# Two attentions reordered: first attention in steps of two tiles with full-row maxima, second attention's transposes one tile later

## The chip, the cores and the metric

The kernel runs on one core of a Trainium2 chip. The metric is the device time of one execution in microseconds (us). Three runs of the kernel before took 2622.91 to 2623.58 us, median 2623.57 us. Engines: TensorE (PE, its weight loads PEld), VectorE (DVE), ScalarE (ACT), GpSimd (POOL) and SyncE (SP), which here issues the DMAs.

## The reference

Two layers, each a cross attention and a feed-forward block, are added to x (16 batches of 56 queries, 256 wide), with a context of 1500 rows of 128 per batch. The two attentions are what the change touches:

```python
    # layer 0: 16 heads of 16; the last 16 context rows go to a second small attention
    q = _ln((x @ Wq + bq).reshape(b, s1, H, HD), qn_w, qn_b)
    k, v = _ln(kv[..., :HD], kn_w, kn_b), kv[..., HD:]
    s = jnp.einsum('bhqd,bhkd->bhqk', q, k) * SCALE
    ctx = jnp.einsum('bhqk,bhkd->bhqd', jax.nn.softmax(s, axis=-1), v)
    # layer 1: 16 heads of 128, rmsnorm on q and k
    scores = jnp.einsum('bqhd,bkhd->bhqk', rmsnorm(q, gq), rmsnorm(k, gk)) * scale
    out = jnp.einsum('bhqk,bhkd->bhqd', jax.nn.softmax(scores, axis=-1), v)
x = x + xattn0(layernorm(x), ctx); x = x + moe(layernorm(x))
x = x + xattn1(layernorm(x), ctx); x = x + bitlinear_ffn(layernorm(x))
```

## The kernel before

The kernel is one program of phases: keys and values of the first attention (and key norms of the second), queries, the first attention (`phase_attention0`), a mixture of experts, the second attention (`phase_attention1`), and a quantised feed-forward block. Each engine has its own instruction stream, written out by hand; semaphores order them. An engine takes its instructions strictly in the written order, so the order of the Python code is the order on the engine. In both attentions one batch is one step; a step has 12 tiles of 128 context rows (`NK`, the last tile is shorter), and 896 columns are the 16 heads times 56 queries, in two halves of 448. fp32 operands are split into a rounded high part and a low rest, so one product of scores is three matmuls per half.

**First attention.** For tile s of batch p, TensorE does six score matmuls into two PSUM banks `sc` (`scores`, lines 1338 to 1340, each half waits until the exp of the tile before has left its bank), ScalarE takes the exp into one of three buffers `pr` (line 1398), and TensorE multiplies the tile two back with the values (`products`, line 1350, 16 heads, 17 columns of weights each). The softmax needs each query's maximum before its scores are made, so while batch p is worked on TensorE computes for batch p+1 a first, coarse product of the rounded queries and keys (`maxima`, line 1312), which VectorE reduces (line 1453). Its 24 matmuls come in 12 groups of two, and the table `PRE` says after which tile's scores which groups stand. Head pairs lie in four sets of 32 rows; each maxima matmul contracts only its own 32 rows, since the queries `QH` are zero in the others. At tile 9 VectorE makes a diagonal of the maxima, TensorE spreads it (`max_rows`, line 1320), and VectorE adds it to the queries (line 1486). ScalarE also rounds batch p+1's keys in three chunks, behind the exps of tiles 0, 1 and 2 (line 1388). The steps run from p = -2 to 16; p = 1 to 12 are a hardware loop over pairs (`Fori`) on every engine, the others are written out (`run`, line 1264).

**Second attention.** For batch b and tile j TensorE makes the scores into a ring of four PSUM banks (`ring`, line 982), VectorE scales them by the key norms into `S` (line 1106) and keeps a running maximum `mx` (lines 1127 and 1130). When tile 11 is done, TensorE transposes `mx` in two parts of 4 and 3 blocks (`maxima`, line 1009), VectorE reduces them (line 1114) and splits them, TensorE spreads them over all rows into two ring banks (`spread`, line 1024), ScalarE copies them to `mb` (line 1173), and GpSimd subtracts them from the 12 tiles (line 1150), ScalarE takes the exps (line 1179), and TensorE multiplies with the context (`output`, line 994). All of this for batch b runs during step b+1, its last six tiles' outputs even in step b+2: at tile j of step b stand, in this order, the scores of b, the first part of the transposes of b-1 (j = 0), an output of b-2 (j < 5), the second part (j = 0), the spreading (j = 1), and an output of b-1 (j > 5). Steps 2 to 13 are a loop over pairs.

The lines that place the maxima of both attentions:

```python
    PRE = {1: (0,), 2: (1, 2), 3: (3,), 4: (4, 5), 5: (6,), 6: (7, 8), 7: (9,), 8: (10, 11)}
    ...
                    if back and j == 0:
                        maxima(0)
                    ...
                    if back and j == 0:
                        maxima(1)
                    if back and j == 1:
                        spread()
```

Of the kernel before, what the change touches and what calls it, by code (L numbers as in the profile page):

```python
# [27 lines left out]
P = 128  # L28
# [5 lines left out]
NK = 12  # L34
# [843 lines left out]
def phase_attention1(nc, g):  # L878
# [15 lines left out]
    with ExitStack() as ctx:  # L894
# [5 lines left out]
        mx, mb = sb("mx", [P, HQ]), sb("mb", [P, HQ])  # L900
# [58 lines left out]
        def _(pe):  # L959
            def step(b, pair, i, front, nxt, back, end):  # L960
                def scores(j):
# [4 lines left out]
                    for half in range(2):  # L966

                        use = 2 * j + half + (2 if j >= 2 else 0)
                        r = (USES * i + use) % RING

                        if use < 4:
                            if from_(b, 1):
                                pe.wait_ge(s_scaled, SC * b - 3 + use)
                        elif use in (8, 9):
                            if from_(b, 1):
                                pe.wait_ge(mb_ready, 2 * (b - 1) + use - 7)
                        else:
                            pe.wait_ge(s_scaled, SC * b + (use - 4 if use < 8 else use - 6) + 1)
# [21 lines left out]
                def maxima(k):  # L1000
# [7 lines left out]
                    for q in range(lo, hi):  # L1008
                        mm = pe.transpose(tb[:, (q - lo) * P:(q - lo + 1) * P], mx[:, q * P:(q + 1) * P], g.ident[:, :])
                    mm.then_inc(mT_ready, 1)  # L1010

                def spread():
# [3 lines left out]
                    for half in range(2):  # L1016
                        if front:
                            pe.wait_ge(s_scaled, SC * b + half + 1)
                        r = (USES * i + 4 + half) % RING
# [51 lines left out]
        def _(dve):  # L1071
# [8 lines left out]

            def step(b, pair, i, front, nxt, back, end):
                for j in range(NK):
# [16 lines left out]
                    if front:  # L1099
                        if from_(b, 2):  # L1100
                            dve.wait_ge(p_used, NK * (b - 2) + j + 1)
                        for half in range(2):
                            r = (USES * i + 2 * j + half + (2 if j >= 2 else 0)) % RING
# [6 lines left out]
                    if back and j == 0:  # L1110

                        for k, (lo, hi) in enumerate(TI):
                            dve.wait_ge(mT_ready, 2 * (b - 1) + k + 1)
                            dve.tensor_reduce(mcol[:, lo:hi],
                                              tb[:, 0:(hi - lo) * P].rearrange("p (a n) -> p a n", n=P),
                                              X, ALU.max).then_inc(mT_taken, 1)
# [6 lines left out]
                    if front:  # L1123

                        dve.wait_ge(s_scaled, SC * b + 2 * j + 2)
                        if j == 0:
                            dve.tensor_copy(mx[:, :], S[i][:, 0, :]).then_inc(mx_ready, 1)
                        else:
                            dve.wait_ge(mx_ready, NK * b + j)
# [1257 lines left out]
```

## Time and profile before

| | |
|---|---|
| median of 3 runs | 2623.57 us |
| profiled execution | 2625.33 us, span 2623.6 us |
| granted TensorE clock, mean | 0.903 of full speed |
| TensorE busy | 2223.8 us (85%) |
| VectorE busy | 1781.6 us (68%) |
| GpSimd busy | 1236.7 us (47%) |
| ScalarE busy | 1187.0 us (45%) |
| first attention, first to last score matmul | about 913 to 1391 us |
| second attention | about 1724 to 2455 us |

The table sums the whole program; its stages have different limits, so each attention is read by itself. Busy time of TensorE is the time in which a matmul is in flight, and matmuls overlap: the distance of two starts is what one costs. A granted clock of 1.00 is 2.4 GHz, 0.50 is 1.2 GHz.

### The profile page before, as it was taken

Reading aid. Unit: us, or ns where it says so; the run is one execution under the profiler, and the core shown is the slowest. Engines: PE = TensorE matmul, PEld = TensorE weight load, DVE = VectorE, ACT = ScalarE, POOL = GpSimd, SP = SyncE. Lnnn points to the kernel's source line nnn. Section 1 sums busy time; section 2 is a strip of 40 time slices with the busy share of each in tenths; the row PEclk is TensorE's granted clock in tenths of the full one; section 3 lists DMA queues with packets and bytes.
Section 4 is the critical chain, followed back from the end, with each engine's and each line's share of the span. In section 5 each row is a group of like instructions: output and inputs, shape, how many; then the busy total and the mean of one; then the engine's idle time right before and its main releaser. Section 6 shows DMA issues by size and latency. Waiting matters only on the chain. (4 is left out here: it accounts for less than half of the span.)

```text
span 2623.6 us, 47067 instructions
## 1 busy us (share of the span) xinstructions
PE 2223.8 (85%) x16760; PEld 1749.7 (67%) x16760; DVE 1781.6 (68%) x2275; ACT 1187.0 (45%) x2007; POOL 1236.7 (47%) x988
## 2 busy tenths in 40 slices
PE   6999999999954599999996776958898989898675
PEld 4887888787832476666674343448888888888543
DVE  5878888888855465555552336968888888887057
ACT  5888888888820154445451123513232323233202
POOL 5666666666510243333330211318686868687300
PEclk9999999999976599999998687979898989899887
DMA  3232323232213133222220622241121212120500
GB/s 99 111 143 109 142 109 142 109 139 113 120 54 86 69 117 113 103 105 103 103 77 31 205 80 75 86 121 50 50 98 49 98 49 98 49 99 20 208 5 14
DMA packets 93876, 246.16 MB, mean 94 GB/s; under 512 B 19409, under 2 KB 65394, under 8 KB 84450
## 3 DMA queue, kind: packets, MB, share of 16 engines
q1 hardware_dynamic: 87602, 231.17, 24.6%
q10 hardware_dynamic: 4608, 9.44, 0.9%
q0 software_dynamic: 1536, 3.67, 0.5%
q8 instruction: 99, 1.62, 0.2%
q14 instruction: 31, 0.25, 0.0%
HBM read 144.25 MB, written 100.01 MB: 93 GB/s over the span
## 5 line engine op out<-in xcount | busy, mean ns | idle before, releaser
L1150 POOL TENSOR_TENSOR a_S<-a_S,a_mb 128x896 f32<-128x896 f32 x192 | 523.2, 2762 | 218.3 <-ACT a_mb L1173 218.3
L317 DVE TENSOR_REDUCE rk<-n_sq 128x1024 f32 (+2 forms) x384 | 465.6, 1213 | 129.3 <-ACT n_sq L255 126.9
L255 ACT ACTIVATE n_sq<-n_slot 128x1024 f32<-128x1024 f32 (+1 forms) x384 | 394.3, 1027 | 140.3 <-PE n_slot L211 131.8
L994 PEld LDWEIGHTS a_ob<-a_y,a_S 128*128 128x128 f32 (+1 forms) x2688 | 346.8, 203 | 6.9 <-issue 1.9
L994 PE MATMUL a_ob<-a_y,a_S 128*128 128x129 f32 (+1 forms) x2688 | 349.8, 286 | 1.7 <-issue 1.7
L209 PE MATMUL n_slot<-n_wh,n_yh 128*128 128x512 f32 (+1 forms) x768 | 318.3, 414 | 25.1 <-POOL n_yl L153 25.1
L1453 DVE TENSOR_REDUCE a_mpart<-a_pre 112x2 f32<-112x1024 f32 (+1 forms) x192 | 219.1, 1178 | 176.1 <-PE a_pre L1312 176.0
L1398 ACT ACTIVATE a_pr<-a_sc 128x448 f32<-128x448 f32 (+1 forms) x384 | 208.3, 544 | 249.7 <-PE a_sc L1340 238.8
L1179 ACT ACTIVATE a_S<-a_S 128x896 f32<-128x896 f32 x192 | 181.1, 950 | 271.1 <-POOL a_S L1150 270.7
L211 PE MATMUL n_slot<-n_wh,n_yl 128*128 128x512 f32 (+1 forms) x768 | 303.7, 395 | 0.0
L210 PE MATMUL n_slot<-n_wl,n_yh 128*128 128x512 f32 (+1 forms) x768 | 302.0, 393 | 0.0
L1130 DVE TENSOR_TENSOR a_mx<-a_mx,a_S 128x896 f32<-128x896 f32 (+1 forms) x176 | 286.8, 1630 | 18.0
L1106 DVE TENSOR_TENSOR a_S<-a_ring,rk 128x448 f32<-128x448 f32 (+1 forms) x384 | 221.6, 612 | 28.8 <-PE a_ring L984 28.8
L183 POOL TENSOR_TENSOR n_khat<-n_kb,n_rs 128x240 f32<-128x240 f32 x192 | 114.3, 595 | 234.5 <-DVE n_rs L332 234.4
L1408 POOL TENSOR_TENSOR a_kl<-a_kT,a_kh 128x1024 fp32r<-128x1024 f32 (+1 forms) x48 | 109.9, 2313 | 213.8 <-ACT a_kh L1388 213.8
L982 PE MATMUL a_ring<-a_Qh,a_yh 128*128 128x448 f32 (+1 forms) x384 | 160.8, 419 | 39.5 <-DVE a_S L1106 24.9
L1338 PE MATMUL a_sc<-a_QM,a_kh 128*128 128x448 f32 (+1 forms) x384 | 164.5, 428 | 19.0 <-issue 18.1
L209 PEld LDWEIGHTS n_slot<-n_wh,n_yh 128*128 128x128 f32 (+1 forms) x768 | 143.1, 186 | 51.3 <-issue 25.0
L211 PEld LDWEIGHTS n_slot<-n_wh,n_yl 128*128 128x128 f32 (+1 forms) x768 | 142.8, 186 | 35.0
L210 PEld LDWEIGHTS n_slot<-n_wl,n_yh 128*128 128x128 f32 (+1 forms) x768 | 143.8, 187 | 26.5
L170 POOL TENSOR_TENSOR n_kb<-n_kb,n_kbias 128x256 f32<-128x256 f32 x192 | 141.6, 737 | 9.7 <-ACT n_kb L269 9.7
L1339 PE MATMUL a_sc<-a_QL,a_kh 128*128 128x448 f32 (+1 forms) x384 | 143.7, 374 | 0.0
(336 smaller groups left out, 4043.6 us busy)
## 6 DMA issues: line engine op xcount, KB each, us to landing
vdram<-n_v SPq DMA_DIRECT2D x16, 1632.0 KB, 5.3
a_v<-vdram SPq DMA_DIRECT2D x16, 1632.0 KB, 6.9
kTdram<-n_kT SPq DMA_DIRECT2D x16, 1484.0 KB, 5.0
a_kT<-kTdram SPq DMA_DIRECT2D x16, 1484.0 KB, 6.5
n_yT<-in_ctxT SPq DMA_DIRECT2D x16, 750.0 KB, 8.9
yhdram<-n_yh SPq DMA_DIRECT2D x16, 750.0 KB, 6.4
yldram<-n_yl SPq DMA_DIRECT2D x16, 750.0 KB, 8.5
a_yh<-yhdram SPq DMA_DIRECT2D x16, 750.0 KB, 6.6
```

The source lines that it names most:

```text
L209: pe.matmul(dst, high, wh[:, cols], start=True, stop=False)
L210: pe.matmul(dst, high, wl[:, cols], start=False, stop=False)
L211: mm = pe.matmul(dst, low, wh[:, cols], start=False, stop=True)
L255: act.activation(sq[0:n, w, :], slot[w][0:n, :], ACT.Square).then_inc(slot_free, 1)
L317: dve.tensor_reduce(g.rk[0:n, b, j, 8 * s:8 * s + 8], sq[0:n, (2 * j + s) % 3, :].rearrange("p (h d) -> p h d", h=8), X, ALU.add)\
L994: mm = pe.matmul(ob[k][:, (q - lo) * (C + 1):(q - lo + 1) * (C + 1)], S[k_][0:n, j, q * P:(q + 1) * P], y1[k_][0:n, j, :], start=(j == 0 a ...
L1106: dve.tensor_tensor(S[i][0:n, j, half * HALF:(half + 1) * HALF].rearrange("p (h q) -> p h q", h=8), ring[r][0:n, 0:HALF].rearrange("p (h q ...
L1130: dve.tensor_tensor(mx[0:n, :], mx[0:n, :], S[i][0:n, j, :], ALU.max).then_inc(mx_ready, 1)
L1150: pool.tensor_tensor(S[1 - i][0:n, j, :], S[1 - i][0:n, j, :], mb[0:n, :], ALU.subtract)\
L1179: act.activation(S[1 - i][0:n, j, :], S[1 - i][0:n, j, :], ACT.Exp).then_inc(p_ready, 1)
L1398: act.activation(pr[0:n, s % 3, unit, :], sc[unit][0:n, 0:HALF], ACT.Exp).then_inc(p_ready, 1)
L1453: dve.tensor_reduce(mpart[:, chunk, k:k + 2], pre[group % 2][0:QP, :, 0:hi - lo], X, ALU.max).then_inc(pre_max, 1)
```

## The change

In the second attention the two parts of the transposes stand one tile later on TensorE, behind the scores of tile 1 (the first ahead of the output, the second behind it), and the spreading stands at tile 2. VectorE reduces them at tile 1. `mx` has two buffers; the copy of tile 0 into it is gone, and the first maximum is taken over tiles 0 and 1 at once, between the two reductions. The ring banks that the spreading takes move two uses on.

In the first attention TensorE's step goes over the tiles in pairs: both tiles' scores, the groups of maxima, then the products of the two tiles before. Three tables (`BETWEEN` the scores, `BEHIND` them, `LAST` behind the products) place the 12 groups. Each maxima matmul contracts all 128 rows. `pr` has four buffers. TensorE's steps are all written out in Python instead of a loop over pairs; the other engines keep theirs. The wait for the shifted queries is made for each half.

```diff
-        mx, mb = sb("mx", [P, HQ]), sb("mb", [P, HQ])
+        mx, mb = two("mx", [P, HQ]), sb("mb", [P, HQ])
...
-                    if back and j == 0:
+                    if back and j == 1:
                         maxima(0)
                     if end and j < LAG:
...
-                    if back and j == 0:
+                    if back and j == 1:
                         maxima(1)
-                    if back and j == 1:
+                    if back and j == 2:
                         spread()
...
+                    if back and j == 1:
+                        reduced(b, 0)
+                    if front and j == 1:
+                        dve.wait_ge(s_scaled, SC * b + 4)
+                        dve.tensor_tensor(mx[i][:, :], S[i][:, 0, :], S[i][:, 1, :], ALU.max).then_inc(mx_ready, 2)
+                    if back and j == 1:
+                        reduced(b, 1)
...
-                        if j == 0:
-                            dve.tensor_copy(mx[:, :], S[i][:, 0, :]).then_inc(mx_ready, 1)
...
-    PRE = {1: (0,), 2: (1, 2), 3: (3,), 4: (4, 5), 5: (6,), 6: (7, 8), 7: (9,), 8: (10, 11)}
+    BETWEEN = {6: (6, 7)}
+    BEHIND = {0: (0, 1), 2: (2, 3), 4: (4, 5), 8: (10, 11)}
+    LAST = {6: (8, 9)}
...
-        pr = sb("pr", [P, 3, 2, HALF])
+        pr = sb("pr", [P, 4, 2, HALF])
...
-                    mm = pe.matmul(pre[group % 2][0:QP, n, 0:hi - lo], QH[i][32 * r:32 * r + 32, half, r * QP:(r + 1) * QP],
-                                   kh[i][32 * r:32 * r + 32, half, lo:hi], start=True, stop=True)
+                    mm = pe.matmul(pre[group % 2][0:QP, n, 0:hi - lo], QH[i][:, half, r * QP:(r + 1) * QP],
+                                   kh[i][:, half, lo:hi], start=True, stop=True)
...
+                for s in range(0, NK, 2):
                     if held(p):
                         scores(p, i, s)
+                    groups(p, i, BETWEEN.get(s, ()))
+                    if held(p):
+                        scores(p, i, s + 1)
...
+                    groups(p, i, BEHIND.get(s, ()))
+                    for j in (s - PV, s - PV + 1):
+                        if s >= PV and held(p):
+                            products(p, i, pair, j)
...
+                    groups(p, i, LAST.get(s, ()))
...
-            run(pe, step)
+
+            for p in range(-2, B + 1):
+                step(p, p % 2, p // 2)
...
-                            if unit == 0 and later(t - 2):
-                                act.wait_ge(p_used, t - 2)
+                            if unit == 0 and later(t - 3):
+                                act.wait_ge(p_used, t - 3)
```

On VectorE in the second attention, at the start of a step, before: `a_S<-a_ring` is the scaling of two halves, `a_mx` the running maximum, `a_mcol<-a_tb` the reduction of a transposed part, `a_mh` and `a_ml` its split.

```order
L1130 TENSOR_TENSOR a_mx<-a_mx,a_S 92x896
L1106 TENSOR_TENSOR a_S<-a_ring,rk 128x448 x2
L1114 TENSOR_REDUCE a_mcol<-a_tb 128x4
L1114 TENSOR_REDUCE a_mcol<-a_tb 128x3
L1120 CAST a_mh<-a_mcol 128x7
L1122 TENSOR_TENSOR a_ml<-a_mcol,a_mh 128x7
L1127 COPY a_mx<-a_S 128x896
L1106 TENSOR_TENSOR a_S<-a_ring,rk 128x448 x2
L1130 TENSOR_TENSOR a_mx<-a_mx,a_S 128x896
```

The same place after the change:

```order
L1132 TENSOR_TENSOR a_mx<-a_mx,a_S 92x896
L1112 TENSOR_TENSOR a_S<-a_ring,rk 128x448 x4
L1084 TENSOR_REDUCE a_mcol<-a_tb 128x4
L1120 TENSOR_TENSOR a_mx<-a_S 128x896
L1084 TENSOR_REDUCE a_mcol<-a_tb 128x3
L1126 CAST a_mh<-a_mcol 128x7
L1128 TENSOR_TENSOR a_ml<-a_mcol,a_mh 128x7
```

The scaling of tile 1 moved ahead of the reductions, the copy is gone, and a maximum stands between the two reductions.

On TensorE in the second attention, a step's start before: `a_ring` are score matmuls (the last half of tile 0), `a_tb` the transposes, `a_ob` an output.

```order
L982 MATMUL a_ring<-a_Qh,a_yh 128x448
L983 MATMUL a_ring<-a_Ql,a_yh 128x448
L984 MATMUL a_ring<-a_Qh,a_yl 128x448
L1004 REGISTER_ALU
L1006 REGISTER_ALU
L1009 MATMUL a_tb<-ident,a_mx 128x128 x4
L990 ISA
L994 MATMUL a_ob<-a_y,a_S 128x129 x7
L1002 ISA
L1009 MATMUL a_tb<-ident,a_mx 128x128 x3
L973 REGISTER_ALU
L982 MATMUL a_ring<-a_Qh,a_yh 128x448
```

After, from the same half of tile 0 on:

```order
L984 MATMUL a_ring<-a_Qh,a_yl 128x448
L990 ISA
L994 MATMUL a_ob<-a_y,a_S 128x129 x7
L973 REGISTER_ALU
L982 MATMUL a_ring<-a_Qh,a_yh 128x448
L983 MATMUL a_ring<-a_Ql,a_yh 128x448
L984 MATMUL a_ring<-a_Qh,a_yl 128x448
L982 MATMUL a_ring<-a_Qh,a_yh 128x448
L983 MATMUL a_ring<-a_Ql,a_yh 128x448
L984 MATMUL a_ring<-a_Qh,a_yl 128x448
L1004 REGISTER_ALU
L1006 REGISTER_ALU
```

An output and the scores of tile 1 now stand between tile 0's scores and the wait for the last maximum; the transposes follow.

On TensorE in the first attention, one tile before: `a_sc` scores, `a_pre` a group of maxima, `a_ob` products, the last row the denominators.

```order
L1338 MATMUL a_sc<-a_QM,a_kh 128x448
L1339 MATMUL a_sc<-a_QL,a_kh 128x448
L1340 MATMUL a_sc<-a_QM,a_kl 128x448
L1338 MATMUL a_sc<-a_QM,a_kh 128x448
L1339 MATMUL a_sc<-a_QL,a_kh 128x448
L1340 MATMUL a_sc<-a_QM,a_kl 128x448
L1307 REGISTER_ALU
L1312 MATMUL a_pre<-a_kh,a_QH 112x512 x2
L1343 REGISTER_ALU
L1350 MATMUL a_ob<-a_pr,a_v 17x56 x16
L1357 MATMUL a_ob<-a_osum,a_den 128x224
```

After, the second tile of a pair up to the denominators:

```order
L1343 MATMUL a_sc<-a_QM,a_kh 128x448
L1344 MATMUL a_sc<-a_QL,a_kh 128x448
L1345 MATMUL a_sc<-a_QM,a_kl 128x448
L1343 MATMUL a_sc<-a_QM,a_kh 128x448
L1344 MATMUL a_sc<-a_QL,a_kh 128x448
L1345 MATMUL a_sc<-a_QM,a_kl 128x448
L1316 MATMUL a_pre<-a_kh,a_QH 112x512 x4
L1355 MATMUL a_ob<-a_pr,a_v 17x56 x32
L1362 MATMUL a_ob<-a_osum,a_den 128x224
```

Two groups of maxima stand in one run, and two tiles' products behind them; the register instructions of the loop are gone.

## Rows read from the trace of the kernel before

**Rows 1.** Stretches: us, then busy us (instructions) of each engine, granted clock, DMA share, GB/s.
```profile
1790.00:2379.00 589.00, 520.63 (x3541) 496.95 (x3542) 498.77 (x623) 187.86 (x224) 438.15 (x159) 0.92 0.20 71
1884.00:1890.00 6.00, 4.36 (x21) 4.37 (x22) 3.27 (x4) 0.95 (x1) 0.56 (x1) 0.50 0.00 0
1032.60:1061.20 28.60, 28.24 (x510) 20.43 (x498) 17.74 (x18) 15.77 (x28) 11.10 (x8) 1.00 0.33 118
```

**Rows 2.** SP's issues in order: start us, us, engine, line, operation, tiles.
```profile
974.72 0.33 SPq L1217 DMA_DIRECT2D a_v<-vdram  x1
...
1286.98 0.33 SPq L1217 DMA_DIRECT2D a_v<-vdram  x1
...
1315.60 0.33 SPq L1217 DMA_DIRECT2D a_v<-vdram  x1
```

**Rows 3.** Waits, first attention: who waited for whom: total us, times, longest.
```profile
PEld a_sc L1338 <- issue: 18.9, 5, 4.1
```

**Rows 4.** TensorE in order, first attention; brackets: idle time before, and its releaser.
```profile
1037.05 0.47 PE L1338 MATMUL a_sc<-a_QM,a_kh 128*128 128x448 f32 x1
1037.36 0.37 PE L1339 MATMUL a_sc<-a_QL,a_kh 128*128 128x448 f32 x1
...
1038.18 0.36 PE L1340 MATMUL a_sc<-a_QM,a_kl 128*128 128x448 f32 x1
1038.47 0.49 PE L1312 MATMUL a_pre<-a_kh,a_QH 32*112 32x512 f32 x4
1038.89 0.59 PE L1350 MATMUL a_ob<-a_pr,a_v 128*17 128x56 f32 x32
1039.41 0.47 PE L1338 MATMUL a_sc<-a_QM,a_kh 128*128 128x448 f32 x1
...
1040.82 0.48 PE L1312 MATMUL a_pre<-a_kh,a_QH 32*112 32x512 f32 x2
...
1057.93 1.06 PE L1320 MATMUL a_pre<-a_dm,a_sel 112*128 112x112 f32 x8
...
1064.88 0.74 PE L1338 MATMUL a_sc<-a_QM,a_kh 128*128 128x448 f32 x1 [3.49 <-issue]
```

**Rows 5.** ScalarE in order, first attention.
```profile
1037.97 1.15 ACT L1398 ACTIVATE a_pr<-a_sc 128x448 f32<-128x448 f32 x2 [0.26 <-PE a_sc L1340]
```

**Rows 6.** TensorE in order, second attention, around a step's start.
```profile
1885.64 1.11 PE L1009 MATMUL a_tb<-ident,a_mx 128*128 128x128 f32 x4 [3.84 <-DVE a_mx L1130]
1886.54 3.22 PE L994 MATMUL a_ob<-a_y,a_S 128*128 128x129 f32 x14
1889.55 0.85 PE L1009 MATMUL a_tb<-ident,a_mx 128*128 128x128 f32 x3
...
1891.56 1.72 PE L994 MATMUL a_ob<-a_y,a_S 128*128 128x129 f32 x14
1893.03 0.31 PE L1024 MATMUL a_ring<-a_identr,a_mh 128*128 128x128 f32 x1
```

**Rows 7.** VectorE in order, second attention, same stretch.
```profile
1883.82 1.69 DVE L1130 TENSOR_TENSOR a_mx<-a_mx,a_S 92x896 f32<-92x896 f32 x1
...
1886.79 0.69 DVE L1114 TENSOR_REDUCE a_mcol<-a_tb 128x4 f32<-128x512 f32 x1 [0.21 <-PE a_tb L1009]
1890.44 0.56 DVE L1114 TENSOR_REDUCE a_mcol<-a_tb 128x3 f32<-128x384 f32 x1 [2.96 <-PE a_tb L1009]
...
1891.32 0.62 DVE L1127 COPY a_mx<-a_S 128x896 f32<-128x896 f32 x1
...
1893.14 1.09 DVE L1130 TENSOR_TENSOR a_mx<-a_mx,a_S 128x896 f32<-128x896 f32 x1
1895.82 1.23 DVE L1106 TENSOR_TENSOR a_S<-a_ring,rk 128x448 f32<-128x448 f32 x2 [1.58 <-PE a_ring L984]
```

**Rows 8.** GpSimd in order, second attention, one batch.
```profile
1851.30 33.26 POOL L1150 TENSOR_TENSOR a_S<-a_S,a_mb 128x896 f32<-128x896 f32 x12 [11.05 <-ACT a_mb L1173]
```

**Rows 9.** Waits, second attention.
```profile
POOL a_S L1150 <- ACT a_mb L1173: 133.3, 12, 11.2
```

More of the change, by code:

```diff
@@ L966, in scores @@
                     for half in range(2):
-                        use = 2 * j + half + (2 if j >= 2 else 0)
+                        use = 2 * j + half + (2 if j >= 3 else 0)
                         r = (USES * i + use) % RING
@@ L1017, in spread @@
                         if front:
-                            pe.wait_ge(s_scaled, SC * b + half + 1)
-                        r = (USES * i + 4 + half) % RING
+                            pe.wait_ge(s_scaled, SC * b + half + 3)
+                        r = (USES * i + 6 + half) % RING
                         for q in range(3 * half, 4 + 3 * half):
@@ L1170, in step @@
                     for half in range(2):
-                        r = (USES * i + 4 + half) % RING
+                        r = (USES * i + 6 + half) % RING
                         act.wait_ge(mb_psum, 2 * (b - 1) + half + 1)
@@ L1324, in prob @@
             def prob(h, j):
-                return pr[:, j % 3, h // 8, (h % 8) * NQ:(h % 8 + 1) * NQ]
+                return pr[:, j % 4, h // 8, (h % 8) * NQ:(h % 8 + 1) * NQ]
             def scores(b, i, j):
@@ L1329, in scores @@
                 if j == 0:
-                    pe.wait_ge(qm_ready, 2 * b + 2)
                     pe.wait_ge(ql_built, 2 * b + 2)
@@ L1334, in scores @@
                 for half in range(2):
+                    if j == 0:
+                        pe.wait_ge(qm_ready, 2 * b + half + 1)
                     if later(2 * t + half - 1):
@@ L1362, in _, with groups @@
             pe.wait_ge(ob_zero, 2)
+            def groups(p, i, which):
+                if held(p + 1):
+                    for group in which:
+                        maxima(p + 1, 1 - i, group)
             def step(p, i, pair):
-                for s in range(NK):
+                for s in range(0, NK, 2):
                     if held(p):
                         scores(p, i, s)
+                    groups(p, i, BETWEEN.get(s, ()))
+                    if held(p):
+                        scores(p, i, s + 1)
                     if s == NK - 2 and held(p + 1):
                         max_rows(p + 1)
-                    if held(p + 1):
-                        for group in PRE.get(s, ()):
-                            maxima(p + 1, 1 - i, group)
-                    if s >= PV and held(p):
-                        products(p, i, pair, s - PV)
-                    if s < PV and held(p - 1):
-                        products(p - 1, 1 - i, pair - 1 + i, s - PV + NK)
-                    if s == PV + 1 and held(p - 1):
+                    groups(p, i, BEHIND.get(s, ()))
+                    for j in (s - PV, s - PV + 1):
+                        if s >= PV and held(p):
+                            products(p, i, pair, j)
+                        if s < PV and held(p - 1):
+                            products(p - 1, 1 - i, pair - 1 + i, j + NK)
+                    groups(p, i, LAST.get(s, ()))
+                    if s == PV and held(p - 1):
                         denominators(p - 1, 1 - i)
-            run(pe, step)
+            for p in range(-2, B + 1):
+                step(p, p % 2, p // 2)
         @block.scalar
@@ L1455, in step @@
             def step(p, i, pair):
-                for s in range(NK):
-                    if held(p + 1):
-                        for group in PRE.get(s, ()):
-                            maximum(p + 1, group)
+                for s in range(0, NK, 2):
                     if s == PV and held(p - 1):
@@ L1467, in step @@
                         dve.reciprocal(rec[:, :], ob[1 - i][:, 4 * NQ:8 * NQ]).then_inc(rec_ready, 1)
-                    if s == NK - 3 and held(p + 1):
+                    if held(p + 1):
+                        for group in BETWEEN.get(s, ()) + BEHIND.get(s, ()) + LAST.get(s, ()):
+                            maximum(p + 1, group)
+                    if s == NK - 2 and held(p + 1):
                         b = p + 1
```

30 lines of the change are left out of this document (14 added, 16 removed).

## The prediction

> **What bounds the kernel now.** I read the table by stretches first, then the chain of waits of the two attentions, then the instructions in order of time. In the second attention no engine is full: TensorE is busy 521 of 589 us and VectorE 499 [rows 1]. POOL's twelve subtractions take 33.26 us behind 11.05 us of idle time, so one batch takes 44.3 us [rows 8]. What closes that cycle is seen around the step's start. VectorE ends the last running maximum of a batch at 1885.51 (1883.82 + 1.69) [rows 7]; TensorE has idled 3.84 us for it [rows 6], then transposes it, runs 14 product matmuls and transposes the rest; VectorE idles 2.96 us for these and 1.58 us for the scores behind them [rows 7]. The reader is to see that VectorE's idle time, not its work, is what is paid, and that TensorE's idle time brings a second price: at 1884 to 1890 the granted clock is 0.50 (1.2 GHz) [rows 1], and 14 product matmuls last 3.22 us there against 1.72 us a few us later [rows 6].
>
> In the first attention TensorE is busy 28.24 of 28.60 us at a granted clock of 1.00 [rows 1]: it is the bound, and each instruction taken from it or added to it counts. A batch takes 28.60 us in the steps written out at the end (1286.98 to 1315.60), but the ten batches from 974.72 to 1286.98 take 312.26 us [rows 2], which is 26 us more than ten times 28.6. The waits say why: five times TensorE waits for nothing that the profile shows, 18.9 us in all [rows 3], and the matmul behind such a wait lasts 0.74 us against 0.47 us elsewhere [rows 3, 4], the lower clock. All five are at the return of TensorE's loop over pairs of batches.
>
> **First attention, loop.** The changed kernel writes TensorE's 19 steps out. The five returns go: -26 us. Code written out as such cost nothing in the last steps (28.60 us), so I charge nothing for it. What is late next is ScalarE's, VectorE's and GpSimd's own loop return, which lay inside TensorE's gap and shows no price there. Ends: 26 us gained, or nothing if another engine's return takes the same time; I take 26, since in the second attention all engines return through loops too, and GpSimd's idle time before a batch is 133.3 us over twelve, 11.2 us the longest [rows 9]: none is longer for a return.
>
> **First attention, order and maxima.** I build a step from the intervals of [rows 4] (start to start):
> - Scores: 0.205 us per matmul ((1038.18 - 1037.36) / 4), 72 of them, 14.8 us, before and after. Coming from products costs 0.10 more (0.31 against 0.205), leaving for another tile shape 0.08 more (0.29 against 0.205). Before, each is paid 12 times, 2.2 us; after, the entry 7 times (the two groups placed behind the products at step 6 pay one) and the exit 6 times, 1.2 us.
> - Products: 0.52 us for a tile's block (1038.89 to 1039.41). Before 12 blocks, 6.2 us. After, two tiles in one run; the second adds 0.52 less a change of shape, about 0.40: 5.5 us.
> - Maxima: before, 32-row matmuls lie beside each other: four last 0.49 us, two 0.48, and the next block starts 0.42 us after them. Eight such blocks cost 3.3 us, and VectorE's reductions hold one up by 0.4 us. After, 24 matmuls of all 128 rows follow each other. No row has this one. The lower end is a quarter of a block of four, 0.10 us; the upper is the 112-column matmul of line 1320, 1.06 us for 8, stretched to 512 columns, 0.61 us. I take the scores' 0.205 us for 448 columns, the same rows and type: 0.23 us at 512, 0.21 us at 460, in all 5.4 us.
> - Maxima rows and denominators: 1.0 and 0.3 us, unchanged.
> - New wait: the second tile's scores stand right behind the first's and use the same two PSUM banks, so they wait for its exp. That starts 0.92 us after the scores and takes 0.55 us [rows 4, 5], so ends at 1.47 us; the second tile would start at 1.34 us. With the load exposed again (0.10 us) that is 0.3 us (ends 0 and 0.4) for five of six pairs (maxima stand between at step 6): 1.4 us. Everything on TensorE is queued behind it, products and maxima too. In the first pair the maxima want the first rounded keys, which ScalarE makes between two exps: 0.3 us.
> Sum before: 14.8 + 2.2 + 6.2 + 3.3 + 0.4 + 1.3 = 28.2 us (28.60 in the trace). Sum after: 14.8 + 1.2 + 5.5 + 5.4 + 1.3 + 1.7 = 29.9 us. A step is 1.4 us longer after keeping part of the 0.4 us that my sum misses; 15 steps carry maxima: +21 us. VectorE's 12 reductions and SP's loads have slack there (VectorE 17.74 of 28.60 us busy [rows 1]), so their later places cost nothing; the fourth probability buffer lets ScalarE run one tile further and is needed for the pairs.
>
> What row tiling is worth bears on this sum. Two 32-row matmuls last as long as four (0.48 and 0.49 us), so half of the blocks used half of it. The Trainium skill (TensorEngine Tiling, Theoretical Speedup) gives up to fourfold for a contraction of 32 or less. By that rule the old maxima would be worth a quarter of 5.4 us, and the edit would cost 4.1 us a step instead of 1.7 us net of the stall; by the rows old blocks cost 3.7 us. The trace does not agree with the full factor, so the sum keeps the rows.
>
> **Second attention.** Times count from the end of the last maximum (1885.51), with the rows of before as durations.
> - Before, VectorE does until tile 2's scaling (1895.82, 10.3 us): scaling of tiles 0 and 1, 1.2 each (1891.94, the copy's end, to 1893.14), reductions 0.69 and 0.56, rounding 0.3 (1891.00 to 1891.32), copy 0.62, maximum 1.09, and idle 0.21 + 2.96 + 1.58; together 10.4 [rows 7].
> - After, TensorE has products and tile 1's scores in the time in which it idled (they need 1.5 us, from 1891.56 to 1893.03, and 6 x 0.205 = 1.2 us, of 3.84), and transposes at once at full clock. VectorE has two scalings (2.4), reduction 0.69, maximum over tiles 0 and 1 (1.09, on the other buffer, so it may stand between the reductions), reduction 0.56, rounding 0.3: 5.0 us without a wait. The copy, 0.62 us, is gone.
> - What is late next: TensorE waits about 1 us for the first reduction before transposing the rest (VectorE is through with it at 3.1 us), then tile 2's scores to 4.9, products 1.5, spreading the maxima (16 small matmuls between 1893.03 and tile 2's scores, which VectorE has at 1895.82, so 1.9 us with 0.9 us for the half tile and its way; it now stands behind tile 2's scores), then tile 3's scores, whose first half is ready at 9.2 us. VectorE would be ready at 7.3 us (5.0 + 1.2 + 1.09) and idles 2 us. Before, tile 3 was scaled at 10.3 + 1.2 + 1.5 = 13.0 us, the 1.5 between the maximum's 1.09 and 1.69, since GpSimd starts in it. A step gains 3.8 us.
> - GpSimd starts at about 9 us instead of 10.1 (1851.30 and one batch of 44.3) and needs 33.3 us of a 40.5 us batch. TensorE is busy 39 of 44.3 us now (521 of 589) and gets back the 3 us or so of its slow stretch (its 14 products alone 1.5 us): some 37 us. Neither is the bound.
> 15 batches (all that have a tile 1 of their own beside maxima of the one before) gain 3.8 us, 57 us. TensorE's gap of 3.84 us becomes two of about 1 us; I take it that the clock stays up, and A is the case in which it doesn't.
>
> **Sum.** -26 + 21 - 57 = -62 us. The profiled execution took 2625.33 us with a span of 2623.6; 2563 us for it. It lies 1.8 us above the runs' median, 2623.57, so about 2561 us.
>
> **Rivals.**
> A, the second attention keeps its slow stretch or its contention. For it: VectorE's maximum is 1.69 us while GpSimd works and 1.09 us while it doesn't [rows 7], and GpSimd starts earlier in the step. If the clock still falls, TensorE's products and spreading take 1.5 to 2 us longer and tile 3 comes as much later; a step gains 1.9 us: 15 x 1.9 less, 2590 us. Against: TensorE's longest gap shrinks to about 1 us. That two-input VectorE work contends with GpSimd is also in the Trainium skill (GPSIMD Engine Reference, Specifications); by that rule, the trace agrees.
> B, the pairs cost nothing: the exp is not late, and a first-attention step comes to 28.4 us. -26 - 3 - 57: 2538 us. Against: 1.47 is over 1.34.
> C, the five returns stay in another form, because ScalarE or VectorE is then late at its own return: 2587 us. For it: before, they return in the shade of TensorE. Against: the second attention, as above.
> D, slower: the 128-row maxima run near the rate of line 1320. Place: the maxima matmuls of the first attention; price 24 of them a step. A step changes by 24 g - 3.9 us for g us each, the saved 83 us are 5.5 us over 15 steps, so from g = 0.39 us on the kernel is slower; at 0.61 us it is 15 x 10.7 - 83 = +78: 2701 us. For it only row 1320; against, the scores at 0.205 us.
> E, no change to be measured: the gain of the second attention needs TensorE's work to move before the wait; if tile 1's scores still ended behind it, only copy and loop would go, -9 - 26 + 21: 2609 us, still faster. Only a mix with D gives no change.
>
> **How the numbers follow.** Forecast 50%, A 18%, B 15%, C 9%, D 3%, E and mixtures 5%. The forecast's own range is 2548 to 2576 (exp wait 0 to 0.4 us, step gain 3.2 to 4.4 us). The range that holds 8 of 10 reaches over most of A, B and C: 2535 to 2593. Faster by over 0.2% (what a measurement of this kernel can tell from none, 5 us): 95%; within: 2%; slower: 3%, which is D.
>
> **What would show it.** In the profile after: SP's value loads of the first attention evenly spaced, about 30 us, none with 5 us more, and no wait of TensorE on nothing; a maxima matmul starting 0.23 us after the one before; a wait of line 1343's weight load for ScalarE's exp of 0.1 to 0.3 us, five a step; in the second attention POOL's starts 40.5 us apart, VectorE's copy gone, its wait for the second transposes near zero, a new one of 2 us for tile 3's scores, and TensorE's clock at 1.00 throughout. Wrong would be: POOL's starts over 42.5 us apart (A), loads with a long interval in each pair (C), maxima matmuls over 0.39 us apart (D).

## The result, and the profile after

Four runs took 2545.13 to 2547.73 us, median 2546.62 us, against 2623.57 us before (runs beside them to 2625.99): ratio 0.9705, 95% interval 0.9688 to 0.9722, or 77 us. The forecast was 2561 us. The profiled execution has a span of 2543.7 us and a mean granted clock of 0.923 (0.903 before). The page's busy times, then two stretches with the columns of [rows 1] (second attention, first attention):

```profile
PE 2206.4 (87%) x16760; PEld 1746.7 (69%) x16760; DVE 1762.5 (69%) x2259; ACT 1183.9 (47%) x2007; POOL 1237.0 (49%) x988
PEclk9999999999976679999999776989999999999876
```

```profile
1790.00:2299.00 509.00, 479.25 (x3449) 453.53 (x3448) 464.08 (x587) 185.80 (x218) 430.30 (x156) 1.00 0.23 83
893.40:1386.00 492.60, 481.19 (x7840) 364.94 (x7840) 286.98 (x288) 243.16 (x429) 173.99 (x125) 0.98 0.29 103
```

Busy times hardly changed; what went is waiting. The clock of the second attention is 1.00 where [rows 1] had 0.92.

**Second attention, −71 us.** From the first to the last rounding of maxima (`mh`) it is 591.3 us instead of 662.3 us. The steps in the loop, measured from one such rounding to the next, are 39.84 us instead of 44.36 us in the mean; the first step went from 45.21 to 37.79 us, the last from 40.5 to 35.91 us. TensorE around a step's start (answers to [rows 6]; repeated score and spreading matmuls left out):

```profile
1899.26 0.66 PE L1009 MATMUL a_tb<-ident,a_mx 128*128 128x128 f32 x4 [0.90 <-DVE a_mx L1132]
1899.75 1.73 PE L994 MATMUL a_ob<-a_y,a_S 128*128 128x129 f32 x14
1901.98 0.55 PE L1009 MATMUL a_tb<-ident,a_mx 128*128 128x128 f32 x3 [0.50 <-DVE a_mcol L1084]
1902.28 0.45 PE L982 MATMUL a_ring<-a_Qh,a_yh 128*128 128x448 f32 x1
...
1903.60 1.72 PE L994 MATMUL a_ob<-a_y,a_S 128*128 128x129 f32 x14
1905.08 0.30 PE L1024 MATMUL a_ring<-a_identr,a_mh 128*128 128x128 f32 x1
...
1906.89 0.42 PE L982 MATMUL a_ring<-a_Qh,a_yh 128*128 128x448 f32 x1
```

The gap of 3.84 us is now 0.90 us and 0.50 us, and the 14 products behind the first transposes last 1.73 us where they lasted 3.22 us. VectorE in the same stretch (answers to [rows 7]):

```profile
1897.48 1.72 DVE L1132 TENSOR_TENSOR a_mx<-a_mx,a_S 92x896 f32<-92x896 f32 x1
1899.13 2.20 DVE L1112 TENSOR_TENSOR a_S<-a_ring,rk 128x448 f32<-128x448 f32 x4
1901.26 0.67 DVE L1084 TENSOR_REDUCE a_mcol<-a_tb 128x4 f32<-128x512 f32 x1
1901.85 1.07 DVE L1120 TENSOR_TENSOR a_mx<-a_S 128x896 f32<-128x896 f32 x1
1902.85 0.54 DVE L1084 TENSOR_REDUCE a_mcol<-a_tb 128x3 f32<-128x384 f32 x1
...
1907.85 1.24 DVE L1112 TENSOR_TENSOR a_S<-a_ring,rk 128x448 f32<-128x448 f32 x2 [1.54 <-PE a_ring L984]
1914.27 0.30 DVE L1097 RECIPROCAL a_rden<-a_ob 128x3 f32<-128x3 f32 x3 [0.60 <-PE a_ob L994]
```

The numbers in brackets are VectorE's idle time before an instruction: neither reduction waits any more. The scaling of tile 3 starts 8.65 us after the last maximum (1899.20) and is what waits now.

**First attention, −9.7 us.** From the first to the last score matmul (of line 1338, now 1343) it is 467.6 us instead of 477.4 us. SP's loads of values (answers to [rows 2]):

```profile
976.95 0.33 SPq L1219 DMA_DIRECT2D a_v<-vdram  x1
1006.69 0.33 SPq L1219 DMA_DIRECT2D a_v<-vdram  x1
1036.46 0.33 SPq L1219 DMA_DIRECT2D a_v<-vdram  x1
...
1274.41 0.33 SPq L1219 DMA_DIRECT2D a_v<-vdram  x1
1304.15 0.33 SPq L1219 DMA_DIRECT2D a_v<-vdram  x1
```

They are 29.76 us apart, every one; before, short ones of 28.6 us alternated with ones some 5 us longer. The wait on nothing of [rows 3] is gone from the table of waits, and the exp's is there:

```profile
PEld a_sc L1343 <- ACT a_pr L1413: 36.2, 94, 0.5
```

TensorE at one pair of tiles (answers to [rows 4]):

```profile
1037.30 0.37 PE L1345 MATMUL a_sc<-a_QM,a_kl 128*128 128x448 f32 x1
1037.77 0.47 PE L1343 MATMUL a_sc<-a_QM,a_kh 128*128 128x448 f32 x1
...
1039.10 1.08 PE L1316 MATMUL a_pre<-a_kh,a_QH 128*112 128x512 f32 x4
1040.11 0.98 PE L1355 MATMUL a_ob<-a_pr,a_v 128*17 128x56 f32 x64
```

The second tile's scores start 0.47 us after the matmul before them, where 0.205 us is the distance without a wait, so the wait for the exp is 0.26 us; the weight load exposed behind it adds 0.10 us. That is so in the first two pairs of a step; in the pairs at tiles 4, 8 and 10 the distance is 0.39 us, a wait of 0.18 us. Four maxima matmuls take 1.01 us to the next start, where four of 32 rows took 0.42 us.

### The profile page after: what moved, and what is told of

Its sections match the earlier page's. It is cut to its first block and busy times, and to the rows that moved or that the text cites. A ratio compares the mean times of both kernels' runs of the same rounds, so it can differ in the third digit from the quotient of the medians.

```text
span 2543.7 us, 46596 instructions
## 1 busy us (share of the span) xinstructions
PE 2206.4 (87%) x16760; PEld 1746.7 (69%) x16760; DVE 1762.5 (69%) x2259; ACT 1183.9 (47%) x2007; POOL 1237.0 (49%) x988
## 3 DMA queue, kind: packets, MB, share of 16 engines
q0 software_dynamic: 1536, 3.67, 0.5%
## 5 line engine op out<-in xcount | busy, mean ns | idle before, releaser
L994 PEld LDWEIGHTS a_ob<-a_y,a_S 128*128 128x128 f32 (+1 forms) x2688 | 325.9, 192 | 8.0 <-issue 1.9
L994 PE MATMUL a_ob<-a_y,a_S 128*128 128x129 f32 (+1 forms) x2688 | 329.3, 276 | 2.3 <-issue 1.7
L1132 DVE TENSOR_TENSOR a_mx<-a_mx,a_S 128x896 f32<-128x896 f32 (+1 forms) x160 | 257.7, 1610 | 16.3
L1343 PE MATMUL a_sc<-a_QM,a_kh 128*128 128x448 f32 (+1 forms) x384 | 158.2, 412 | 3.6
L984 PE MATMUL a_ring<-a_Qh,a_yl 128*128 128x448 f32 (+1 forms) x384 | 142.6, 371 | 0.0
```

The lines of the kernel that those rows point to most:

```text
L994: mm = pe.matmul(ob[k][:, (q - lo) * (C + 1):(q - lo + 1) * (C + 1)], S[k_][0:n, j, q * P:(q + 1) * P], y1[k_][0:n, j, :], start=(j == 0 a ...
L1132: dve.tensor_tensor(mx[i][0:n, :], mx[i][0:n, :], S[i][0:n, j, :], ALU.max).then_inc(mx_ready, 1)
```

## The experiments

Ratios are to the kernel before, run beside them, with 95% intervals.

**e1: the second attention's part alone.** The first attention as before, `PRE`, three `pr` buffers, 32 rows and the loop included.

```diff
-    BETWEEN = {6: (6, 7)}
-    BEHIND = {0: (0, 1), 2: (2, 3), 4: (4, 5), 8: (10, 11)}
-    LAST = {6: (8, 9)}
+    PRE = {1: (0,), 2: (1, 2), 3: (3,), 4: (4, 5), 5: (6,), 6: (7, 8), 7: (9,), 8: (10, 11)}
...
-        pr = sb("pr", [P, 4, 2, HALF])
+        pr = sb("pr", [P, 3, 2, HALF])
...
-            for p in range(-2, B + 1):
-                step(p, p % 2, p // 2)
+            run(pe, step)
```

> The kernel before with the second attention of the changed one; the first attention is untouched. Theory (the two parts add up, and the second attention is the larger): in the changed kernel's trace the second attention is shorter by some 71 us between its first and last rounding of the maxima (1746.41 to 2337.73 against 1757.17 to 2419.46), so 2553 us, ratio 0.973; POOL's starts 39.8 us apart, and the first attention unchanged, with five waits of TensorE at the loop's return. Rival (the gain of the second attention is the 57 us that I forecast, and the rest came from somewhere else): 2566 us.

2555.73 us, 0.9736 [0.9719, 0.9753]; batches of the second attention 39.84 us, as in the whole change. So the two parts add up without disturbing each other, and the second attention gives about 70 of the 77 us.

**e2: the loop's removal alone.**

```diff
-            run(pe, step)
+            for p in range(-2, B + 1):
+                step(p, p % 2, p // 2)
```

> The kernel before with only TensorE's steps of the first attention written out instead of the loop; the order, the 32-row maxima and the three buffers stay. Theory (the loop's return costs 5.2 us five times, and nothing else returns late): 2623.6 - 26 = 2597.5 us, batches 28.6 us apart throughout. Rival (another engine's return takes its place): at most some us gained, 2620 us. Second rival (the loop is not what the changed order lost or won): a time between, with intervals over 29 us at every second batch.

2599.02 us, 0.9899 [0.9883, 0.9916], 26.2 us less than the 2625.20 us of the kernel before beside it; the first attention takes 449.4 us instead of 477.4 us. The loads of values:

```profile
974.73 0.33 SPq L1217 DMA_DIRECT2D a_v<-vdram  x1
1003.23 0.33 SPq L1217 DMA_DIRECT2D a_v<-vdram  x1
1031.71 0.33 SPq L1217 DMA_DIRECT2D a_v<-vdram  x1
```

Each step takes 28.49 us, and nothing else of the change is in this kernel: the returns of TensorE's loop cost some 5 us each, and those of the other engines' loops, which stayed, leave no long interval.

**e3: the change with maxima of 32 rows.**

```diff
-                    mm = pe.matmul(pre[...], QH[i][:, half, r * QP:(r + 1) * QP],
-                                   kh[i][:, half, lo:hi], ...)
+                    mm = pe.matmul(pre[...], QH[i][32 * r:32 * r + 32, half, r * QP:(r + 1) * QP],
+                                   kh[i][32 * r:32 * r + 32, half, lo:hi], ...)
```

> The changed kernel with the maxima back on 32 rows each, in the new places (four of them side by side). Theory (the 128-row maxima are what makes a step of the first attention 1.2 us longer, and pairs are a gain by themselves): six blocks of two groups cost 0.42 us and a change of shape each, about 3.1 us a step instead of 5.8, so a step is 27.1 us instead of 29.8, 15 x 2.6 = 39 us less: 2508 us, ratio 0.956 to before. Rival (the reductions on VectorE hold the groups up once they come earlier): a step of 28 to 29 us, 2520 to 2535 us. Rival (four tiles side by side don't run side by side in this place): 2546 us, no change.

2508.67 us, 0.9557 [0.9541, 0.9573]; a step of the first attention 27.23 us instead of 29.76 us.

```profile
1031.51 0.49 PE L1316 MATMUL a_pre<-a_kh,a_QH 32*112 32x512 f32 x4
1031.93 0.98 PE L1355 MATMUL a_ob<-a_pr,a_v 128*17 128x56 f32 x64
```

Four lie beside each other and take 0.42 us to the products, instead of 1.01 us; coming from the scores costs 0.29 instead of 0.21 us (1031.22 to 1031.51 and 1038.89 to 1039.10), so a block behind scores saves 0.51 us. By the traces the blocks behind the scores save 0.65, 0.50, 0.50 and 0.36 us, the one behind the products 0.53 us, and the one between scores only 0.16 us: it has a change of shape on either side, and takes 0.60 us and not 0.42 us for a reason that was not traced. With 0.1 us lost at the maxima rows that makes up the 2.53 us. Steps in pairs are worth 28.49 − 27.23 = 1.26 us, and the full-row maxima take twice that back: this part of the change makes the kernel slower by 38 us than it could be.

More than half of these 1.26 us is a wait that the pairs no longer have. In the order of before, one block of maxima in each step waits for VectorE's reductions; in the kernel before:

```profile
1048.26 0.48 PE L1312 MATMUL a_pre<-a_kh,a_QH 32*112 32x512 f32 x2
1049.10 0.46 PE L1312 MATMUL a_pre<-a_kh,a_QH 32*112 32x460 f32 x2 [0.36 <-DVE a_mpart L1453]
```

This block takes 1.24 us to the products (1049.50), and 1.16 us in e2, where the others take about 0.42 us; in e3 no block takes more than 0.60 us.

**e4: the change with four blocks of maxima between the scores.**

```diff
-    BETWEEN = {6: (6, 7)}
-    BEHIND = {0: (0, 1), 2: (2, 3), 4: (4, 5), 8: (10, 11)}
+    BETWEEN = {2: (2, 3), 4: (4, 5), 6: (6, 7), 8: (10, 11)}
+    BEHIND = {0: (0, 1)}
```

> The changed kernel with three more groups of 128-row maxima between the scores of a pair (at tiles 2, 4 and 8) instead of behind them. Theory (the second tile's scores wait 0.26 us for the exp of the first, and the exposed load is part of it): three of these waits in a step go, 0.8 us, 15 steps, 12 us less: 2535 us; VectorE's reductions may give back 0.3 us a step at tile 8. Rival (the wait lies in the shade of something else): 2546 us.

2537.48 us, 0.9669 [0.9653, 0.9685]; step 29.24 us, −0.52 us where −0.8 us was expected. TensorE:

```profile
1037.70 1.07 PE L1316 MATMUL a_pre<-a_kh,a_QH 128*112 128x512 f32 x4
1038.62 0.36 PE L1343 MATMUL a_sc<-a_QM,a_kh 128*128 128x448 f32 x1
```

Maxima of 128 rows between scores cost 0.92 us for four, 0.23 us each, and the exp ends beneath them. Scores and maxima together fall at tiles 2 and 3 from 3.92 to 3.57 us and at tiles 4 and 5 from 3.91 to 3.63 us, which is the wait for the exp with the exposed load. At tiles 8 and 9 they rise from 3.67 to 3.80 us, since the block stands earlier there and its second half waits for VectorE's reductions:

```profile
1140.06 0.57 PE L1316 MATMUL a_pre<-a_kh,a_QH 128*112 128x460 f32 x2
1140.81 0.67 PE L1316 MATMUL a_pre<-a_kh,a_QH 128*112 128x460 f32 x2 [0.18 <-DVE a_mpart L1468]
```

−0.35 − 0.28 + 0.13 = −0.50 us is the step's gain. Two of the three blocks gave about what was expected, and the third gave nothing, for the reason that the expectation named as possible.

**e5: both, 32 rows and between the scores.** e3 with the tables of e4.

> The changed kernel with 32-row maxima and three more groups between a pair's scores. Theory (a 32-row group in the pair covers the exp wait of 0.26 us but brings two changes of tile shape of about 0.1 us each in a place that had none): nearly no gain over the 2508.7 us of the pairs with 32 rows, 2503 to 2509 us. Rival (the waits covered add in full, as with the 128-row groups, 9 to 10 us): 2499 us.

2514.75 us, 0.957 [0.9547, 0.9593]; the interval overlaps that of e3, but the trace tells them apart: a step is 27.63 us, 0.40 us longer than in e3, where no difference was expected. The loss is not at the added changes of tile shape. Scores and maxima together take 3.42 us at tiles 2 and 3 in both kernels, and 3.32 us instead of 3.41 us at tiles 4 and 5: there the changes of shape cost about what the covered wait is worth, as expected. At tiles 8 and 9 they take 3.94 us instead of 3.31 us. As in e4, the block comes before VectorE's reductions have freed its bank, and its second half starts 0.70 us behind the first:

```profile
1128.52 0.47 PE L1316 MATMUL a_pre<-a_kh,a_QH 32*112 32x460 f32 x2
1129.22 0.47 PE L1316 MATMUL a_pre<-a_kh,a_QH 32*112 32x460 f32 x2 [0.24 <-DVE a_mpart L1468]
```

What one change of shape costs was not measured alone.

**e6: the copy of tile 0 kept.** The change, with the copy and a maximum at tile 1 in place of the one over both tiles.

```diff
+                    if front and j == 0:
+                        dve.wait_ge(s_scaled, SC * b + 2)
+                        dve.tensor_copy(mx[i][:, :], S[i][:, 0, :]).then_inc(mx_ready, 1)
```

> The changed kernel, but in the second attention VectorE copies tile 0 to the running maximum as before (0.62 us) and takes the maximum with tile 1 over the copy; everything else is the changed kernel's. Theory (VectorE is on the path from one batch's last maximum to the next): the copy's 0.55 us come back in each batch, but at tile 3 VectorE waits 1.54 us for TensorE, and of a copy ahead of the reductions part is swallowed there only if the scores don't move with it; the spreading waits for the reductions, so they move with it: +0.5 us in 15 batches, 2546.6 + 8 = 2555 us. Rival (the 1.54 us of idle time swallow it): 2547 us.

2570.48 us, 0.979 [0.9769, 0.9812]: 24 us slower than the change, three times what was expected. VectorE, then TensorE:

```profile
1946.37 1.14 DVE L1112 TENSOR_TENSOR a_S<-a_ring,rk 128x448 f32<-128x448 f32 x2
1947.54 1.33 DVE L1120 COPY a_mx<-a_S 128x896 f32<-128x896 f32 x1
1948.80 1.14 DVE L1112 TENSOR_TENSOR a_S<-a_ring,rk 128x448 f32<-128x448 f32 x2
1949.86 0.67 DVE L1084 TENSOR_REDUCE a_mcol<-a_tb 128x4 f32<-128x512 f32 x1
```

```profile
1950.59 0.55 PE L1009 MATMUL a_tb<-ident,a_mx 128*128 128x128 f32 x3 [1.80 <-DVE a_mcol L1084]
```

The copy lasts 1.33 us, not the 0.62 us of [rows 7], and TensorE's wait for the first reduction grows by as much, from 0.50 to 1.80 us. The batch grows by 1.37 us, to 41.21 us. In the moved order the copy stands on the path, and beside GpSimd's last subtractions, which end at 1948.38 us in this trace; in [rows 7, 8] it stood between GpSimd's batches. Two of the batches take 42.85 us. In each of them the clock falls again; in the first behind TensorE's wait of 1.87 us, which ends at 1907.75:

```profile
1904.00:1916.00 12.00, 10.13 (x67) 9.68 (x66) 8.47 (x15) 2.04 (x3) 2.45 (x2) 0.86 0.00 0
```

The second attention is 22.7 us longer than in the change, 3.3 us of it from these two batches and the rest some 1.4 us in each of the 14. The move with the copy kept still shortens the second attention by 48 us (662.3 to 614.0 us); taking the copy out gives the other 23 of the 71 us.

**e7: before, with TensorE kept busy in the gap.** 16 matmuls, overwritten by the transposes, stand ahead of them. Order, waits and copy are those of before.

```diff
+                    if front and back and j == 0:
+                        ...
+                        for _ in range(WARM):
+                            pe.matmul(tb[:, 0:HALF], yh[i][:, 0:P], Qh[i][:, 0:HALF], start=True, stop=True)
```

> The kernel before with 16 score-like matmuls whose result is overwritten, put on TensorE in the second attention behind tile 0's scores, in the 3.84 us in which it waits for the last maximum. They do not change the order and hold nothing up (3.3 us). Theory (part of the old step's cost is the clock that falls in that gap, not the order): the granted clock stays at 1.00, 14 products last 1.7 us instead of 3.2 and the transposes half as long, VectorE's wait of 2.96 us shrinks to 1.2 us, a batch is 42.5 us instead of 44.3 and 15 batches give 25 to 28 us: 2596 us. Rival (the clock is of no account there, the whole gain is the order): 2623 us. Rival (the order brings nothing beside the clock): 2555 us.

2591.73 us, 0.9868 [0.9848, 0.9889]; a batch 42.02 us, −2.34 us.

```profile
1850.00:2300.00 450.00, 433.01 (x3058) 411.26 (x3056) 403.37 (x503) 153.98 (x184) 362.27 (x131) 1.00 0.22 79
```

```profile
1876.32 3.43 PE L1048 MATMUL a_tb<-a_Qh,a_yh 128*128 128x448 f32 x16
1880.31 0.66 PE L1010 MATMUL a_tb<-ident,a_mx 128*128 128x128 f32 x4 [0.57 <-DVE a_mx L1136]
1880.81 1.73 PE L995 MATMUL a_ob<-a_y,a_S 128*128 128x129 f32 x14
```

TensorE waits for VectorE as before, but its clock stays at 2.4 GHz and the work behind the wait has its full speed: this alone gives 34 us. Of the change's 4.52 us a batch, 2.34 us can so be had through the clock alone, and 2.18 us need the new order without the copy. By e6 the copy would cost 1.37 us of these, which leaves some 0.8 us for the order itself (41.21 us with the copy kept, against 42.02 us); that is an estimate, since the parts need not add up.

**e8: an output moved later.** e3, with the output of tile 2's place done behind tile 3's scores.

```diff
-                        for t in ((NK - LAG - 1 + j,) if j < LAG - 1 else (NK - 2, NK - 1)):
+                        for t in ((6,), (7,), (), (8, 9), (10, 11))[j]:
```

> The changed kernel with 32-row maxima (2508.7 us) and, in the second attention, the output that stands ahead of the spreading at tile 2 moved behind tile 3's scores. Theory (VectorE's 1.54 us of idle time before tile 3 is this output's 1.47 us on TensorE): a batch is 38.4 us instead of 39.8, 14 to 15 of them give 20 us: 2489 us. Rival (TensorE, busy 479 of 509 us, is the bound by then and the output comes back at tile 4): 2500 to 2508 us.

2525.32 us, 0.9614 [0.9593, 0.9635], 17 us slower than e3 where 19 us faster was expected; a batch 40.74 us. The reading behind it, that tile 3's scaling ends the path, fell. From the first transposes (1907.19) to VectorE's normalisation at tile 5 (1922.65) it is 15.46 us, against 15.01 us in the change (1899.26 to 1914.27). Apart from short waits for VectorE (0.50 us ahead of the second transposes in the change; 0.43 us there and 0.18 us ahead of the spreading in e8), TensorE works through this stretch, and VectorE waits for it at the end (0.60 us in the change; 0.20 us or nothing in e8, where VectorE itself is nearly as late). So what TensorE has to do between the transposes and the normalisation sets the end; moving an output inside the stretch takes nothing out of it. The move even made the stretch longer, by 0.45 us of the 0.89 us that a batch gained in length: the output had stood ahead of the spreading and hidden VectorE's split, and without it the spreading starts some 0.3 us late (1911.24 to 1911.79 from the last score matmul). The rest is behind the normalisation, where VectorE's maximum takes 2.04 us for 1.55 us in e3; the one ahead of it takes 2.15 us for 1.66 us. GpSimd starts about 1.1 us earlier behind the last maximum in e8; that this makes them longer was not tried.

**e9: an output moved into the waits.** That reading tells how to gain: take an output out of the stretch. e3, with output 7 ahead of the first transposes, 8 between the two parts, none at tile 2.

```diff
+                    if end and j == 1:
+                        output(b - 2, 7, i)
                     if back and j == 1:
                         maxima(0)
...
+                        for t in ((6,), (8,), (), (9,), (10, 11))[j]:
```

> As e3 (maxima in pairs of 32 rows), and in the second attention output 7 stands before the first part of tile 1's transposes, 8 between the two parts, none at tile 2, 9 at tile 3, and 10 and 11 at tile 4. Theory that TensorE's own work from the transposes to the normalisation sets the period, and that the two gaps around the transposes (0.90 and 0.50 us, waits for VectorE's maxima) can hold part of it: 1.5 us leaves the path, the period falls from 39.84 to about 38.3 us, 14 intervals, 22 us: 2486 us. Rival, that the transposes come later by what the outputs last beyond the gaps and the rest of the step moves with them: no gain, 2508 us or slower.

2493.89 us, 0.9501 [0.9485, 0.9517], the fastest of all; a batch 38.73 us, −1.12 us. TensorE:

```profile
1901.62 1.72 PE L994 MATMUL a_ob<-a_y,a_S 128*128 128x129 f32 x14
1903.18 0.60 PE L1009 MATMUL a_tb<-ident,a_mx 128*128 128x128 f32 x4
1903.61 1.73 PE L994 MATMUL a_ob<-a_y,a_S 128*128 128x129 f32 x14
1905.40 0.55 PE L1009 MATMUL a_tb<-ident,a_mx 128*128 128x128 f32 x3
...
1907.35 0.32 PE L1024 MATMUL a_ring<-a_identr,a_mh 128*128 128x128 f32 x1 [0.18 <-DVE a_ml L1130]
```

Both waits are gone. From the last maximum's end (1902.62 us in this trace) the second part starts at 2.78 us, as in the change (1901.98 − 1899.20), though the first starts 0.5 us later than there: VectorE is busy scaling anyway, and the output ahead of the first part was free. The spreading starts at 4.73 instead of 5.88 us, 1.15 us earlier. It now waits 0.18 us for the split on VectorE, part of why 1.12 us came and not 1.5 us. 14 x 1.12 = 15.7 us agrees with the 14.8 us between the medians.

**e10: two outputs between the parts.** As e9, with 7 and 8 both between.

```diff
+                        for t in ((6,), (7, 8), (), (9,), (10, 11))[j]:
```

> As e3, and outputs 7 and 8 both stand between the two parts of tile 1's transposes, none at tile 2, 9 at tile 3, 10 and 11 at tile 4. By the theory of e9 the gap between the two parts (0.50 us) holds a third of one output, and the second part starts about 0.7 us later, so half of the gain is lost: period 38.9 to 39.2 us, 2495 us. Rival as for e9: 2508 us or slower. If both beat e3 and this one less, the gap before the first part is what the output fills.

2504.03 us, 0.9544 [0.9528, 0.956]; a batch 39.29 to 39.37 us. This is half of e9's gain a batch, a little less than was expected (38.9 to 39.2 us, and 2495 us in all): a second output behind the first transposes pushes the second part, and the gap ahead of the first stays empty. The time is 4.6 us under e3's, for 14 x 0.5 = 7 us; the intervals of the two ratios overlap, so by the medians alone it could not be told from e3.

## Why the prediction was right, and where it was off

The likeliest case was the right one, 77 us against 62 us; the time lies in the range, and 1.4 us under the forecast's own range of 2548 to 2576 us. That inner range was drawn too narrow for what it names: five exp waits of 0 to 0.4 us and a step gain of 3.2 to 4.4 us, over 15 steps each, reach from about 2531 to 2578 us. The steps, each with its size:

- **The loop, −26 us.** Shown by e2: −26.2 us. Rival C, that the returns stay in another form, is out.
- **Order and maxima of the first attention, +21 us.** The step rose by 29.76 − 28.49 = 1.27 us, or 19 us over 15, for a forecast of 1.4 us. The stage agrees: from first to last score matmul it lost 28.0 us with the loop (477.4 to 449.4 us, e2) and took 18.2 us back (467.6 us). The maxima matmul is 0.23 us (e4), the value taken between 0.10 and 0.61 us, and rival D needed 0.39 us. The exp's wait with the exposed load is 0.36 us in two pairs and 0.2 to 0.3 us in the other three, for 0.3 us, and the maxima behind the second tile change shape into the products for 0.09 us a block. What the sum had wrong is a term of before: the block that VectorE's reductions hold up costs 1.24 us instead of 0.42 us (the lines are at e3), a stall of 0.8 us and not of 0.4 us. That is the 0.4 us by which the sum of 28.2 us missed the 28.60 us of the trace. Rival B, no cost of the pairs, is right in the pairs and wrong in the sum: the pairs gain (e3), the 128 rows cost more.
- **Second attention, −57 us.** The mechanism held at each point: transposes behind tile 1's scores, no wait for the second part, a wait for tile 3's scores. Its size was too small, −71 us. The forecast had the first reduction done at 3.1 us after the last maximum; it was done at 2.65 us (1901.85), since four scalings in a row take 2.2 us and not 2.4, and everything behind it moved up: tile 3 at 8.65 us for 9.2 us. That is 0.55 of the 0.7 us a step that the forecast missed; in the kernel before, tile 3 came at 13.13 us (1898.64) for 13.0 us, which is the other 0.13 us. In 15 steps this makes 10 us; most of the 4 us that are left is the first batch, which gained 7.4 us.
- **Rival A, the clock or the contention stays.** The clock is 1.00, as the case against A had it. Its price was 1.9 us a step for the slow stretch; taking that stretch out of the kernel before gave 2.34 us (e7), and in e6 a batch in which the clock fell was 1.64 us longer than its neighbours. The maximum ahead of the transposes lasts 1.72 us as before (1.69 us), with GpSimd still at work until 1901.15 us (1869.92 and 31.23 us):

```profile
1869.92 31.23 POOL L1152 TENSOR_TENSOR a_S<-a_S,a_mb 128x896 f32<-128x896 f32 x11
1907.72 18.74 POOL L1152 TENSOR_TENSOR a_S<-a_S,a_mb 128x896 f32<-128x896 f32 x7 [6.57 <-ACT a_mb L1175]
```

- **What is late next.** The forecast named tile 3's scores for VectorE, with an idle time of 2 us. VectorE does wait there, 1.54 us, but e8 shows that this wait alone does not set the batch: TensorE's work from the transposes to tile 5 does. The copy was priced at its 0.62 us of [rows 7] as saved time; e6 shows 1.33 us, for kept in the new order it would have stood beside GpSimd.

Row tiling was priced by the rows at 3.7 us for the old blocks (stall included) against 5.4 us for the new ones. With the stall as measured the old blocks cost 4.1 us, and full blocks of four 32-row matmuls, which the pairs allow everywhere, cost 2.6 us in six (e3: 0.39 to 0.60 us each). By the Trainium skill (TensorEngine Tiling, Theoretical Speedup) a contraction of 32 or less can gain up to fourfold; the trace shows a gain of 2.2, from 0.23 to 0.105 us a matmul (0.42 us for four), within that bound and about half of it. Half of the old blocks held two matmuls, which lasted as long as four; that hid what full blocks are worth, and what the edit gave away.

## What to carry to other kernels

TensorE, waiting 3.84 us for another engine here, paid twice, since its clock fell: measure the clock right behind each wait. Where nothing useful can be put in the wait, work that is thrown away can keep the clock up; here it gave half of what the new order gave (e7). A block of work that is moved earlier can meet a wait that its old place hid, as the maxima at tile 8 did (e4, e5); and one that is moved away can uncover one, as the output ahead of the spreading did (e8). When work is moved ahead of a wait, ask which operations of the waited-for engine now stand beside a third engine (the copy, 0.62 to 1.33 us), and take them off the path. To find what sets a pipelined step, move one piece within it and one piece out of it: only the second shortened this one (e8, e9).

## What the runs showed of the hardware

- Four matmuls of 32 rows in the four row groups lasted 0.49 us, and two 0.48 us [rows 4]; four of 32 rows take 0.42 us to the next start, four of 128 rows 0.92 us between matmuls of the same shape and 1.01 us ahead of the 17-column ones.
- A copy of 128x896 fp32 on VectorE, one input and one output, lasted 0.62 us while GpSimd was idle and 1.33 us while it worked (e6). The maximum with two inputs goes from 1.09 to between 1.53 and 1.83 us; in e8 two of a batch last over 2 us.
- Sixteen matmuls of 448 columns in a gap of 3.84 us, ending 0.57 us before the awaited transposes, kept the clock at 2.4 GHz throughout (e7). With gaps of 0.90 and 0.50 us in a batch it stayed there in the whole loop (the change); with gaps of about 1.0 and 1.8 us it fell in two of the batches (e6).
- The return of TensorE's loop cost some 5 us a time in the first attention, of which 3.49 us show as idle [rows 4]. Whether it is the length of the loop's body that makes this was not tried.
